# Narrowing the stationary operand of the layer-1 score terms from 128 to 72 columns

## The reference

```python
h = relu(layernorm(x))
x = x + gat2(elu(gat1(h)))            # two graph-attention layers
h = relu(layernorm(x))
x = x + h + h @ sum(weights).T + bias[adj].sum(axis=2)

def gat_layer(x, mask, W, a_src, a_dst, bias, concat):
    xl = (x @ W).reshape(B, N, H, F)              # layer 1: 4 heads of 128
    asrc = einsum('bnhf,hf->bnh', xl, a_src)      # the score terms
    adst = einsum('bnhf,hf->bnh', xl, a_dst)
    e = leaky_relu(asrc[:, :, None, :] + adst[:, None, :, :], 0.2)
    attn = softmax(where(mask, e, -1e9), axis=1)
    return einsum('bsdh,bshf->bdhf', attn, xl) (+ bias)
```

## Time and profile before

| | us |
|---|---|
| median of 3 runs | 532.21 (531.6 to 533.09) |
| profiled execution, its own time | 532.61 |
| span of its profile | 530.9 |
| PE busy / PEld busy | 492.1 / 424.0 |
| DVE busy | 492.0 |
| ACT busy / POOL busy | 419.5 / 402.1 |

### The profile page before, as it was taken

One profiled execution on the slowest core, in us unless ns is written; L12 is line 12 of the kernel. 1 busy time (PEld: TensorE's weight loads), 2 busy tenths in 40 slices (PEclk: granted clock), 3 DMA queues, 4 the chain that ended last, 5 costly groups with the idle time before them and its releaser, 6 DMA issues.

```text
span 530.9 us, 14794 instructions
## 1 busy us (share of the span) xinstructions
PE 492.1 (93%) x3398; PEld 424.0 (80%) x3398; DVE 492.0 (93%) x1495; ACT 419.5 (79%) x1603; POOL 402.1 (76%) x557
## 2 busy tenths in 40 slices
PE   0478899999999999999999999999999999999875
PEld 0356788888898888888898888888898888888653
DVE  6978999999999999999999999999999999999862
ACT  3167798987898888888898888988889888888741
POOL 3837698887787888778787887878787888887542
PEclk9969999999999999999999999999999999999995
DMA  8301111111111111110111111111111110001001
GB/s 236 91 31 34 31 33 32 53 54 31 43 50 51 51 44 38 51 51 28 43 50 51 51 49 32 50 51 37 35 50 51 51 51 2 21 23 42 22 22 41
DMA packets 29893, 24.62 MB, mean 46 GB/s; under 512 B 2085, under 2 KB 29225, under 8 KB 29866
## 3 DMA queue, kind: packets, MB, share of 16 engines
q1 hardware_dynamic: 29154, 23.01, 14.2%
q10 hardware_dynamic: 712, 1.32, 0.9%
HBM read 15.34 MB, written 8.39 MB: 45 GB/s over the span
## 4 chain that ended last, share of the span: by engine, by line
DVE 43%; issue 27%; PE 14%; POOL 6%; ACT 3%; DVEq 3%; DMA 2%; SPq 1%; ACTq 0%; POOLq 0%
DVE L L705 5%; DVE h L724 5%; DVE nmax L710 3%; DVE bn L769 3%; DVE elu_e L718 3%; DVE xl L701 3%; DVE x_all L779 2%; DVE hn L682 2%; DMA x_all<-in_x 2%; DVE h2n L689 2%; DVE L L745 2%; DVE top_label L662 1%; DVE bn L636 1%; PE pA L873 1%; DVE ab L730 1%
## 5 line engine op out<-in xcount | busy, mean ns | idle before, releaser
L331 POOL TENSOR_TENSOR h_lo<-h,h_hi 128x512 fp32r<-128x512 f32 x64 | 81.7, 1276 | 36.7 <-ACT h_hi L497 36.7
L445 ACT ACTIVATE L<-L,nmax 128x128 f32<-128x128 f32 x256 | 100.5, 418 | 0.3 <-DVE nmax L710 0.3
L497 ACT ACTIVATE h_hi<-h 128x512 fp32r<-128x512 f32 x64 | 40.5, 633 | 52.2 <-DVE h L724 52.1
L347 POOL TENSOR_TENSOR P<-L,rsum 128x512 f32<-128x512 f32 x64 | 71.2, 1113 | 13.4 <-DVE rsum L714 13.1
L354 POOL TENSOR_TENSOR hT_lo<-hT_f,hT_hi 128x256 fp32r<-128x256 f32 x64 | 48.4, 756 | 41.5 <-ACT hT_hi L428 41.5
L885 PE MATMUL pY<-w_hi,h_hi 128*128 128x258 f32 x256 | 78.0, 305 | 0.6 <-ACT xl L503 0.6
L887 PE MATMUL pY<-w_hi,h_lo 128*128 128x258 f32 x256 | 72.6, 283 | 0.0
L886 PE MATMUL pY<-w_lo,h_hi 128*128 128x258 f32 x256 | 72.5, 283 | 0.0
L873 PEld LDWEIGHTS pA<-PT,xl 128*128 128x128 f32 x512 | 66.9, 191 | 4.8 <-ACT PT L453 1.3
L873 PE MATMUL pA<-PT,xl 128*128 128x128 f32 x512 | 67.6, 275 | 0.5 <-ACT PT L453 0.5
L445 ACT ACTIVATION_READ_ACCUMULATOR L<-L,nmax 128x1 f32 x256 | 55.5, 217 | 0.0
(11 more groups left out here) (138 smaller groups left out, 1739.9 us busy)
## 6 DMA issues: line engine op xcount, KB each, us to landing
x_all<-in_x SPq DMA_DIRECT2D x32, 256.0 KB, 2.8
out<-x_all SPq DMA_DIRECT2D x32, 256.0 KB, 2.2
adj_all<-in_adj SPq DMA_DIRECT2D x32, 128.0 KB, 2.6
rhs<-lhs SPq DMA_DIRECT2D x128, 4.0 KB
rhs<-lhs SPq DMA_DIRECT2D x64, 1.0 KB
x_all<-in_L_gnn_W ACTq DMA_DIRECT2D x1, 512.0 KB, 5.0
x_all<-in_L_gnn_W SPq DMA_DIRECT2D x1, 512.0 KB, 8.5
x_all<-in_L_gnn_weights SPq DMA_DIRECT2D x2, 256.0 KB, 9.7
```

What stands on the lines that cost most here:

```text
L331: pool.tensor_tensor(h1_lo[p][:, :, :].rearrange("p a b -> p (a b)"), h1[p][:, :], h1_hi[p][:, :, :].rearrange("p a b -> p (a b)").bitcast ...
L347: pool.tensor_tensor(P1[p][:, :, :], L1[p][:, :, :], rsum1[p][:, :].unsqueeze(2).broadcast_to([128, H, 128]), ALU.mult).then_inc(s_P1, 1)
L445: last = act.activation(L1[p][:, h, :], L1[p][:, h, :], ACT.Exp, bias=nmax1[p][:, h:h + 1], accum_out=sum1[p][:, h:h + 1])
```

## The change

The tile of the folded columns has 72 columns instead of 128, and the four matmuls write rows 0 to 71 of `pH` instead of 0 to 127. The memset of the tile covers 288 elements per partition instead of 512, and tiles allocated after it lie 896 bytes earlier in each partition. The order of the instructions on every engine is the same.

```diff
-        w1_att_cols = sb("w1_att_cols", [128, KD, 2, 128], F32R)
+        w1_att_cols = sb("w1_att_cols", [128, KD, 2, CW], F32R)
...
                 for k in range(KD):
-                    pe.matmul(pH[:, 0:128], w1_att_cols[:, k, 0, :], hT_hi[p][:, k, :], start=(k == 0), stop=False)
-                    mm = pe.matmul(pH[:, 0:128], w1_att_cols[:, k, 1, :], hT_lo[p][:, k, :], start=False, stop=(k == KD - 1))
+                    pe.matmul(pH[0:CW, 0:128], w1_att_cols[:, k, 0, :], hT_hi[p][:, k, :], start=(k == 0), stop=False)
+                    mm = pe.matmul(pH[0:CW, 0:128], w1_att_cols[:, k, 1, :], hT_lo[p][:, k, :], start=False, stop=(k == KD - 1))
                 mm.then_inc(s_R1, 1)
```

## The result

The changed kernel took 528.78 us (median of 8 runs, 526.86 to 530.38) against 532.49 (median of 8, 531.6 to 533.33). The ratio formed from the runs is 0.9917, 95% interval 0.9897 to 0.9937: 0.8% faster, about 4.4 us, where 2.6 us were forecast from the median. The two medians alone are 3.7 us apart, a ratio of 0.9930. The range of the prediction, 528.2 to 532.4 us, reached down to 0.9925 of the median that it started from. The direction and the path were as forecast, but the path works in two slots of four where the prediction counted on one, and the size was too small.

A forecast was written before the change was run, and what follows sets the result against it. DVE was taken to set the pace, with late PE (L895) delaying it through ACT and POOL at L759. Savings of 2.25 (stretched slots) + 0.3 (neighbours) + 0.35 (start) = 2.9 us gave 529.6 us, range 528.2 to 532.4.

The forecast's parts named there:

- 0.15 us less on PE per graph: Four matmuls ahead of L895: three steps paced by the weight load each get 0.05 us shorter; bounds 0 to 0.23.
- The once-in-four slot with the long L759: Slot like that at 304: L354 moves and L759 ends 0.15 us earlier, 15 times, 2.25 us.
- The neighbour slot: Slot like that at 290: L682 holds L354, L759 gains 0.03 us, ten or eleven times, 0.3 us.
- Four slots: Sign of being right: the program's four-slot repeat gets 0.15 to 0.2 us shorter.
- The start, -0.35: Two graphs on the path to L694 at the low clock: up to 0.56 us to be had, 0.35 counted.
- The end, nothing: After 485 us there are no score terms, so no gain was counted.
- a rival of the slower side: Pattern slips: one more long L718 costs 0.9 us, three or more over 0.3%; all slower forms together 0.10.
- hidden anyway: Chain through L354 is re-timed by something else; only start and early part gain, 531.0 to 531.9 us; with small saving 0.30.
- no saving on PE: Moving fp32r operand paces the steps, so the narrow operand saves nothing: 532.2 us; chance of nothing saved 0.08.
- POOL overtaking L682: Slot at 290: L354 goes first and L682 waits 0.73 us for it, about 541 us; all slower forms 0.10.
- the lost fast path: Fast loads need 128 columns, so 72-column loads get slower and L759 0.15 us later: 534.5 us, 2 in 100.
- L759's stretch goes altogether: L354 moves far enough that L759 keeps 0.25 us: 5.5 us gained, 526.5; with better pattern 0.06.

The follow-up runs named there:

- parity pair: Changed kernel with the transpose of P2 made twice, for even graphs in one kernel and odd in the other: 532.07 us and 529.87 us.
- rotated pair: Kernel before and changed kernel, each with DVE's list rotated so the loop's branch precedes residual1's wait for PE: 532.88 us and 528.97 us.
- norm_late_before: Kernel before (128 columns) with normalise2 (L759) placed behind stats1 in DVE's list: 529.15 us, ratio 0.9914 to the kernel before.
- w72_wide_tile: Kernel before with only the four matmuls narrowed to 72 columns, the tile still 128 wide in memory: 528.56 us, ratio 0.9925.
- dup_p2_even: Changed kernel with the transpose of P2 made twice for even graphs: 532.07 us, ratio 0.9981 to the kernel before.
- rot_before: Kernel before (128 columns) with DVE's list rotated, moving only the loop's branch ahead of residual1's wait for PE: 532.88 us, ratio 1.0004.
- w100: Kernel before with the four matmuls reading 100 columns, the tile still 128 wide: 531.35 us, ratio 0.9967.
- w16: Kernel before with the four matmuls reading 16 columns, the tile still 128 wide: 526.37 us, ratio 0.9880.

## Why the prediction was right in kind and too small

- **DVE sets the pace, PE reaches it through ACT and POOL at L759**: right. The parity pair and the rotated pair show it. It isn't "the only" path: the one over L913 and DVE's branch lies within 0.07 us of it in one slot, and what L347 does to L718 weighs as much (norm_late_before).
- **0.15 us less on PE per graph**: right; 0.14 at the four matmuls, and 0.18 and 0.12 at L895 in the two slots shown.
- **The once-in-four slot with the long L759**: forecast 0.47 and 0.15 gained, measured 0.51 and 0.12.
- **The neighbour slot, "L682 runs until 289.87 and L354 can't start before; I count 0.03"**: the step that failed. The slot gained 0.17 per four slots in the mean, over some ten turns about 1.5 us that I had not counted. Both halves of the step are wrong. L354 follows ACT's L428 and not L682, as the rotation shows. And L682 doesn't stay: DVE's 0.27 us of idle time ahead of it was no fixed cost, since L736 follows the end of PE's L913 by 0.84 us; in the changed kernel both are 0.17 earlier and the gap is 0.10 to 0.12. I took the small stretch of L759 (0.32 against 0.25) for the whole of the wait; the rest had only been spent a little earlier.
- **Four slots**: forecast 0.15 to 0.2 shorter, measured 0.29.
- **The start, -0.35**: not to be seen, +2.13 in the profiled execution, with the clock's low stretch at another place; +0.22 in w72_wide_tile.
- **The end, nothing**: one slot near 440 us fell the other way. L718 there took 1.26 before and 0.42 after, with L347 stretched in its place:

```profile
440.78 1.12 POOL L347 TENSOR_TENSOR P<-L,rsum 128x512 f32<-128x512 f32 x1 [0.40 <-DVE rsum L714]
440.92 1.26 DVE L718 TENSOR_SCALAR elu_e<-elu_e 128x512 f32<-128x512 f32 x1
```

```profile
439.57 1.46 POOL L347 TENSOR_TENSOR P<-L,rsum 128x512 f32<-128x512 f32 x1 [0.41 <-DVE rsum L714]
439.71 0.42 DVE L718 TENSOR_SCALAR elu_e<-elu_e 128x512 f32<-128x512 f32 x1
```

With normalise2 in its old place, the same slot is short in all profiles with 72 or 16 columns but that of dup_p2_even, and long in those with 128 or 100. The prediction had such a flip as a rival of the slower side only. That slot and the next are 0.6 us shorter together. The last 0.9 us of the profiled pair lie behind the last L724, where the low clock also falls differently. They are not the narrow operand's: from the last L724 to the end it is 22.3 us before and 21.4 after, but 21.4 in rot_before with its 128 columns too.
- **Rivals**: hidden anyway, no saving on PE, and POOL overtaking L682 are all refuted by the measured time; the lost fast path by w100 and w16. That L759's stretch goes altogether was not had by narrow loads, but by the reorder, and there it wasn't what gained the time.

## What to carry to other kernels

A stationary operand padded with zero columns costs load time for the padding too, and with a moving operand of 128 columns that time was not hidden here. When two engines both look full, look for a slot in which an instruction ends just when another engine's does: that end may be in the loop, however small the stretch looks, since idle time just ahead of it may cover the rest. Test such a loop by adding a tenth of a microsecond in every second slot, and check in the trace that the instruction meant to be late is late. Before you credit a reorder to the instruction that you moved, compare the others: here the gain of the reorder lay in another one.

## What the runs showed of the hardware

The mean load was 97 ns for 16 columns, 147 for 72, 171 for 100 and 197 (L838) for 128, so nearly linear, some 0.9 ns per column on top of about 83. Four matmuls of 128 moving columns with such loads took 0.23, 0.26, 0.32 and 0.40 us to the start of the next instruction. The Trainium skill (TensorE: Matmul & The Clock Gate, section LDWEIGHTS) gives columns / 1.2 ns, 0.83 ns per column. The slope measured here agrees; the 83 ns on top are in these rows only.

A short DVE instruction and a POOL instruction that overlap can stretch each other, whichever way round: L718 took 1.26 us beside an L347 of 1.12, or 0.42 beside an L347 of 1.46.

Where TensorE's granted clock fell at the start differed from profile to profile (24 to 36 us, 36 to 45 us, or not between 24 and 50), with 2 us between the outcomes; what decides it stayed open.
